# Four-layer graph and expert network on one core: the mask of an attention layer added by matmuls, its key and output rows handled in halves, and the order of the next layer's weight splits moved

## The reference, cut to what matters

```
x = x + gnn_L(layernorm(x));  x = x + ffn_L(layernorm(x))       (L = 0..3)
```

```
q, k, v = h @ Wq, h @ Wk, h @ Wv
score[t, s] = q[t] . k[s] / sqrt(64)     per head, for the edges s -> t; softmax over the edges of t
a = softmax-weighted sum of v;  o = a @ Wo
m = layernorm(h + o) * g1 + b1;  out = layernorm(m + relu(m @ W1 + b1') @ W2 + b2') * g2 + b2
```

## Time and profile before

| what | value |
|---|---|
| time, three runs | 580.49 us median (578.05 to 582.21) |
| the profiled execution | 578.05 us, of which its span is 576.3 us |
| TensorE busy | 549.3 us, 95% of the span |
| VectorE busy | 501.2 us, 87% |
| ScalarE busy | 428.2 us, 74% |
| GpSimd busy | 105.9 us, 18% |
| granted TensorE clock, mean | 0.997 of full speed |

### The profile page before, as it was taken

The page is one execution under the profiler, slowest core; times in us unless marked ns, Lnnn a source line. Parts: engine busy times, 40 slices in busy tenths (PEclk is TensorE's granted clock), DMA queues, the critical chain, the costliest instruction groups (busy, mean ns, idle before and its releaser), DMA issues.

```text
span 576.3 us, 8408 instructions
## 1 busy us (share of the span) xinstructions
PE 549.3 (95%) x2743; PEld 447.1 (78%) x2743; DVE 501.2 (87%) x486; ACT 428.2 (74%) x440; POOL 105.9 (18%) x82
## 2 busy tenths in 40 slices
PE   5898999999999999799999999999998999999997
PEld 4575888887688887588888888888877787888886
DVE  6789899897768886899999999999987769998996
ACT  5697898983268766978989899898843468878783
POOL 3132333000100003344343534410000200000000
PEclk9998999999999999999999999999999999999999
DMA  7889899998238885689999999999892258999920
GB/s 286 332 309 424 300 359 358 348 366 310 74 143 320 318 317 180 252 324 353 364 355 355 355 350 354 343 367 356 335 373 90 77 215 309 337 367 366 350 93 19
DMA packets 27978, 170.06 MB, mean 295 GB/s; under 512 B 5338, under 2 KB 5467, under 8 KB 7980
## 3 DMA queue, kind: packets, MB, share of 16 engines
q1 hardware_dynamic: 25986, 166.72, 76.3%
q10 hardware_dynamic: 1968, 3.04, 1.7%
HBM read 169.49 MB, written 0.26 MB: 295 GB/s over the span
## 4 chain that ended last, share of the span: by engine, by line
PE 80%; DVE 9%; ACT 6%; issue 3%; POOL 2%; DVEq 0%; POOLq 0%; ACTq 0%
PE y L678 34%; PE pre L678 33%; PE tp L684 5%; DVE w_lo L1068 4%; ACT w_hi L409 3%; PE wt L698 2%; PE y L779 1%; POOL rstd L345 1%; ACT L472 1%; DVE st L1015 1%; PE wt L909 1%; PE y L786 0%; PE tp L691 0%; PE pre L795 0%; ACT h L472 0%
## 5 line engine op out<-in xcount | busy, mean ns | idle before, releaser
L1068 DVE TENSOR_TENSOR w_lo<-raw,w_hi 128x2048 fp32r<-128x2048 f32 x151 | 354.2, 2368 | 31.9 <-ACT w_hi L409 30.7
L409 ACT ACTIVATE w_hi<-raw 128x2048 fp32r<-128x2048 f32 x152 | 287.7, 1916 | 0.0
L477 ACT ACTIVATE hT_hi<-tp 128x512 fp32r<-128x512 f32 x66 | 39.4, 598 | 58.2 <-PE tp L684 58.2
L678 PE MATMUL y<-w_hi,hT_hi 128*128 128x512 f32 x280 | 81.7, 413 | 0.0
L678 PE MATMUL pre<-w_hi,x_hi 128*128 128x512 f32 x292 | 79.7, 394 | 1.9 <-ACT x_hi L422 1.7
L678 PE MATMUL pre<-w_lo,x_hi 128*128 128x512 f32 x292 | 79.4, 394 | 1.2 <-DVE w_lo L1068 1.1
L678 PE MATMUL pre<-w_hi,x_lo 128*128 128x512 f32 x292 | 79.2, 393 | 0.2
L678 PE MATMUL y<-w_lo,hT_hi 128*128 128x512 f32 x280 | 75.8, 392 | 0.7 <-DVE w_lo L1068 0.6
L678 PE MATMUL y<-w_hi,hT_lo 128*128 128x512 f32 x280 | 75.2, 390 | 0.0
L678 PEld LDWEIGHTS pre<-w_lo,x_hi 128*128 128x128 f32 x292 | 55.1, 190 | 14.1 <-DVE w_lo L1068 1.9
L678 PEld LDWEIGHTS pre<-w_hi,x_hi 128*128 128x128 f32 x292 | 53.8, 188 | 14.8 <-issue 3.6
(11 more groups left out here) (267 smaller groups left out, 454.6 us busy)
## 6 DMA issues: line engine op xcount, KB each, us to landing
raw<-in_chunks SPq DMA_DIRECT2D x156, 1024.0 KB, 4.9
bias_wide<-in_L_ffn_b SPq DMA_DIRECT2D x4, 256.0 KB, 11.7
bias_wide<-in_L_ffn_b ACTq DMA_DIRECT2D x4, 256.0 KB, 6.3
side<-in_L_gnn_emb ACTq DMA_DIRECT2D x1, 512.0 KB, 4.1
affine<-in_L_ffn_W SPq DMA_DIRECT2D x1, 512.0 KB, 7.3
side<-in_L_ffn_W SPq DMA_DIRECT2D x1, 512.0 KB, 10.2
affine<-in_L_gnn_ln_g ACTq DMA_DIRECT2D x2, 256.0 KB, 5.8
affine<-in_L_gnn_ln_b ACTq DMA_DIRECT2D x2, 256.0 KB, 7.4
```

The source lines that it names most:

```text
L409: act.activation(w_hi[:, g % SPLIT_SLOTS], raw[:, g % RAW_SLOTS], ACT.Copy).then_inc(w_hi_ready, 4)
L477: act.activation(hT_hi[:, (s - 1) % 2], tp[:].rearrange("p (c n) -> p c n", n=P), ACT.Copy).then_inc(hT_hi_ready, 1)
L678: last = pe.matmul(dst, xs[:, k], ws[:, k], start=start and i == 0, stop=stop and i == len(passes) - 1, skip_group_check=seeded)
L1068: dve.tensor_tensor(w_lo[:, i], raw[:, g % RAW_SLOTS], w_hi[:, i].bitcast(F32), ALU.subtract).then_inc(w_lo_ready, 4)
```

## The change

What it does: (1) VectorE adds epsilon to the variance, behind `bn_aggr`, in every norm, and GpSimd only takes the power. (2) The number of clock keepers at layer 1's graph norm goes from 30 to 20. (3) q is scaled by 1/8 when ScalarE copies it; the mask `pen`, now float32r, is put into the two score banks by one matmul each with a float32r identity, and the score matmuls add to it; VectorE takes maximum and difference straight from the banks, which are now `pre[0]` and `wt[0]`. (4) k is copied, turned and copied back in two halves of columns, into two banks; the 6 keepers behind it are gone. (5) The score matmuls stand inside the v product, behind its first 4 matmuls. (6) The second bank of attended rows is divided in two halves, and the rows are turned, rounded and split by halves; the 3 keepers there are gone. (7) VectorE no longer splits parts of F between the scores and the attended rows: F's first quarter is split behind the last division, the other three behind the remainder of the turned rows, F+1 whole behind the first norm, and F+2 behind the last. (8) ScalarE rounds the second half of F+1 and both of F+2 ahead of the turned sum, not behind it. (9) One 128x128 copy for the float32r identity, in layer 1.

```diff
-BRIDGE = {"l0g": 0, "l0f": 0, "l1g": 30, "l1f": 37, "l2g": 23, "l2f": 30, "l3g": 28, "l3f": 14}
+BRIDGE = {"l0g": 0, "l0f": 0, "l1g": 20, "l1f": 37, "l2g": 23, "l2f": 30, "l3g": 28, "l3f": 14}
...
-                pool.wait_ge(sm("var"), nth("var", tag))
-                link(pool.tensor_scalar(rstd[:, 0:1], mv[:, 1:2], LN_EPS, None, ALU.add))
+                pool.wait_ge(sm("var_eps"), nth("var", tag))
...
-            act.activation(h[:, 0], pre[0][:], ACT.Copy).then_inc(sm("l3g_q"), 1)
+            act.activation(h[:, 0], pre[0][:], ACT.Copy, scale=DK ** -0.5).then_inc(sm("l3g_q"), 1)
             act.wait_ge(chunk_done, G_L3G + 2)
-            act.activation(h[:, 1], pre[1][:], ACT.Copy).then_inc(sm("l3g_k"), 1)
+            for cols in COL_HALVES:
+                act.activation(h[:, 1, cols], pre[1][:, cols], ACT.Copy).then_inc(sm("l3g_k"), 1)
...
-            round_turned("l3g_aT", tp, hT_hi[:, 0], "l3g_aThi")
+            round_halves("l3g_aT", hT_hi[:, 0], "l3g_aThi")
             round_half(G_L3F + 1, 0)
+            round_half(G_L3F + 1, 2)
+            round_half(G_L3F + 2, 0)
+            round_half(G_L3F + 2, 2)
             round_halves("l3g_midT", XT, "l3g_midTs")
-            round_half(G_L3F + 1, 2)
             act.wait_ge(sm("l3g_f1"), 1)
             act.activation(fT[0:32, :], ms[0:32, 0:P], ACT.Relu, bias=l3b1[:, 0:1]).then_inc(sm("l3g_f1s"), 1)
-            round_half(G_L3F + 2, 0)
-            round_half(G_L3F + 2, 2)
...
-            pe.wait_ge(sm("l3g_k"), 1)
-            turn(y[1], h[:, 1], sm("l3g_kT"))
-            keep_clock(6)
-            pe.wait_ge(sm("l3g_qTs"), 1)
-            pe.wait_ge(sm("l3g_kTs"), 1)
-            for j in range(HEADS // 2):
...
-            product(G_L3G + 2, y[0][:], x_hi, x_lo, True, True)
+            pe.wait_ge(sm("ident_r"), 1)
+            for dst in scored:
+                pe.matmul(dst[:].rearrange("p (c n) -> p c n", n=P), ident_r[:],
+                          pen[:].unsqueeze(1).broadcast_to([P, 4, P]), start=True, stop=True)
+            for part in range(2):
+                pe.wait_ge(sm("l3g_k"), part + 1)
+                for c in range(2):
+                    col = (2 * part + c) * P
+                    last = pe.transpose(k_turned[part][:, c * P:(c + 1) * P], h[:, 1, col:col + P], ident[:])
+                last.then_inc(sm("l3g_kT"), 1)
+
+            def scores():
+
+                pe.wait_ge(sm("l3g_qTs"), 1)
+                for j in range(HEADS // 2):
+                    if j % 2 == 0:
+                        pe.wait_ge(sm("l3g_kTs"), j // 2 + 1)
...
+            product(G_L3G + 2, y[0][:], x_hi, x_lo, True, True, between=scores)
...
-            pe.wait_ge(sm("l3g_a"), 2)
-            turn(tp, h[:, 0], sm("l3g_aT"))
-            keep_clock(3)
-            pe.wait_ge(sm("l3g_aThi"), 1)
-            product(G_L3G + 3, pre[1][:], hT_hi[:, 0], hT_lo[:, 0], True, True, low=(sm("l3g_aTlo"), 1))
+            for part in range(2):
+                pe.wait_ge(sm("l3g_a"), part + 2)
+                turn_half(h[:, 0], part, sm("l3g_aT"))
+            product(G_L3G + 3, pre[1][:], hT_hi[:, 0], hT_lo[:, 0], True, True, low=(sm("l3g_aTlo"), 2),
+                    high=(sm("l3g_aThi"), 1))
...
                 dve.bn_aggr(mv[:], st[:]).then_inc(sm("var"), 1)
+                dve.wait_ge(sm("var"), nth("var", tag))
+                dve.tensor_scalar(rstd[:, 0:1], mv[:, 1:2], LN_EPS, None, ALU.add).then_inc(sm("var_eps"), 1)
...
+            dve.tensor_copy(ident_r[:], ident[:]).then_inc(sm("ident_r"), 1)
...
-            dve.wait_ge(sm("l3g_kT"), 1)
-            dve.tensor_copy(scratch[:, 3 * D:4 * D], y[1][:]).then_inc(sm("l3g_kTs"), 1)
-            split_part(G_L3F, 0, 2)
+            for part in range(2):
+                dve.wait_ge(sm("l3g_kT"), part + 1)
+                dve.tensor_copy(scratch[:, 3 * D + part * 2 * P:3 * D + (part + 1) * 2 * P],
+                                k_turned[part][:, 0:2 * P]).then_inc(sm("l3g_kTs"), 1)
...
-                link(dve.scalar_tensor_tensor(out=S[:, hs], in0=chunks4(pre[p]), scalar=DK ** -0.5,
-                                              in1=pen[:].unsqueeze(1).broadcast_to([P, 4, P]), op0=ALU.mult,
-                                              op1=ALU.add))
-                link(dve.reduce_max(row[:, 0, hs], S[:, hs], AX_X))
-                dve.tensor_tensor(S[:, hs], S[:, hs], row[:, 0, hs].unsqueeze(2).broadcast_to([P, 4, P]),
+                link(dve.reduce_max(row[:, 0, hs], chunks4(scored[p]), AX_X))
+                dve.tensor_tensor(S[:, hs], chunks4(scored[p]), row[:, 0, hs].unsqueeze(2).broadcast_to([P, 4, P]),
                                   ALU.subtract).then_inc(sm("l3g_centred"), 1)
...
-                dve.tensor_tensor(h[:, 0].rearrange("t (j p d) -> t p j d", p=2, d=DK)[:, p], sums[:, :, 0:DK],
-                                  row[:, 3, hs].unsqueeze(2).broadcast_to([P, 4, DK]), ALU.mult).then_inc(
-                    sm("l3g_a"), 1)
-                split_part(G_L3F, 2 + p, 1)
-            low_turned("l3g_aThi", tp, hT_hi[:, 0], hT_lo[:, 0], "l3g_aTlo")
-            split_part(G_L3F + 1, 0, 2)
+                weighed = h[:, 0].rearrange("t (j p d) -> t p j d", p=2, d=DK)[:, p]
+                for js in [slice(0, 4)] if p == 0 else [slice(0, 2), slice(2, 4)]:
+                    dve.tensor_tensor(weighed[:, js], sums[:, js, 0:DK], row[:, 3, hs][:, js].unsqueeze(2).broadcast_to(
+                        [P, js.stop - js.start, DK]), ALU.mult).then_inc(sm("l3g_a"), 1)
+            split_part(G_L3F, 0, 1)
+            low_halves("l3g_aThi", hT_hi[:, 0], hT_lo[:, 0], "l3g_aTlo")
+            split_part(G_L3F, 1, 3)
...
-            split_part(G_L3F + 1, 2, 2)
+            split_part(G_L3F + 1, 0, 4)
...
-            split_part(G_L3F + 2, 0, 1)
...
-            split_part(G_L3F + 2, 1, 1)
             normalise_x("l3f")
-            split_part(G_L3F + 2, 2, 2)
+            split_part(G_L3F + 2, 0, 1)
             low_x("l3f")
+            split_part(G_L3F + 2, 1, 3)
             split_part(G_L3F + 3, 0, 4)
```

More of the change, by code:

```diff
@@ L175, in gnn_ffn_kernel @@
         agg2 = sb("agg2", [P, P])
-        pen = sb("pen", [P, P])
+        pen = sb("pen", [P, P], F32R)
+        ident_r = sb("ident_r", [P, P], F32R)
         mat_a = sb("mat_a", [P, P])
@@ L219, in gnn_ffn_kernel @@
         turned = [tp, wt[0]]
+        k_turned = [y[1], ms]
+        scored = [pre[0], wt[0]]
         landed = [sm(f"landed{i}") for i in range(RAW_SLOTS)]
@@ L661, in _, with product @@
         def _(pe):
-            def product(g, dst, xs_hi, xs_lo, start, stop, it=None, seeded=False, low=None, high=None):
+            def product(g, dst, xs_hi, xs_lo, start, stop, it=None, seeded=False, low=None, high=None, between=None):
                 hi, lo = w_hi[:, g % SPLIT_SLOTS], w_lo[:, g % SPLIT_SLOTS]
@@ L677, in product @@
                         pe.wait_ge(low[0], low[1])
+                    if i == KC and between is not None:
+                        between()
                     last = pe.matmul(dst, xs[:, k], ws[:, k], start=start and i == 0,
@@ L934, in _ @@
             turn(tp, h[:, 0], sm("l3g_qT"))
-            pe.wait_ge(sm("l3g_k"), 1)
-            turn(y[1], h[:, 1], sm("l3g_kT"))
-            keep_clock(6)
-            pe.wait_ge(sm("l3g_qTs"), 1)
-            pe.wait_ge(sm("l3g_kTs"), 1)
-            for j in range(HEADS // 2):
[L941 to L945, removed]
-            product(G_L3G + 2, y[0][:], x_hi, x_lo, True, True)
+            pe.wait_ge(sm("ident_r"), 1)
[13 more added lines that the diff above has]
+                        pe.wait_ge(sm("l3g_kTs"), j // 2 + 1)
+                    for p in range(2):
+                        rows = slice(p * DK, (p + 1) * DK)
+                        last = pe.matmul(scored[p][:, j * P:(j + 1) * P],
+                                         scratch[rows, 2 * D + j * P:2 * D + (j + 1) * P],
+                                         scratch[rows, 3 * D + j * P:3 * D + (j + 1) * P], start=False, stop=True,
+                                         skip_group_check=True)
+                last.then_inc(sm("l3g_scores"), 1)
+            product(G_L3G + 2, y[0][:], x_hi, x_lo, True, True, between=scores)
             def turn_exps(p):
@@ L1243, in graph_matrices @@
                     dve.memset(row[:, 5, :], 1.0)
-                    link(dve.tensor_scalar(pen[:], c_ds[:], 1.0, None, ALU.min))
-                    link(dve.tensor_scalar(pen[:], pen[:], -MASKED, MASKED, ALU.mult, ALU.add))
+                    link(dve.tensor_scalar(mat_b[:], c_ds[:], 1.0, None, ALU.min))
+                    link(dve.tensor_scalar(pen[:], mat_b[:], -MASKED, MASKED, ALU.mult, ALU.add))
                     link(dve.tensor_scalar(row[:, 3, 3:4], scal[:, 2:3], 1.0, None, ALU.add))
```

## The result

| | before | changed |
|---|---|---|
| median of 12 runs each | 581.5 us (578.05 to 583.55) | 577.19 us (574.14 to 579.78) |
| ratio, with its 95% interval | | 0.994 (0.9917 to 0.9964) |
| profiled execution, span | 578.05 us, 576.3 | 576.84 us, 575.0 |
| mean granted clock of the profiled execution | 0.997 | 0.994 |

The forecast was 576.6 us with a range of 573.2 to 579.8 and a change of 0.7%. The measured change is 0.6%. It lies within 1%, as forecast, and its interval, 0.4% to 0.8% faster, lies clear of no change.

The account below looks back on a forecast made before the run. TensorE, busy 95% of the span at full clock, was taken to bound the kernel; only stretches between products could shorten. Terms 0.30 + 0.70 + 0.37 + 2.56 = 3.93 us put the median at 576.6 us, range 573.2 to 579.8.

Parts of the forecast that it names:

- Norms: Epsilon on VectorE: five norms on the chain gain 0.14 us each, 0.70 together; for all norms, ends 0 and 1.9.
- Layer 0's first: First norm of layer 0: GpSimd's whole add step goes, since the variance is long known; gain 0.30 us.
- The norm inside the attention: First norm in the attention: the power is held beside a two-SBUF-input VectorE operation and still ends 0.44 behind; gain 0.
- Layer 1's graph norm: 30 keepers cut to 20: turning starts about 0.5 us earlier, but x_lo limits the third pass; gain 0.37, ends 0.1 and 0.65.
- Scores: Attention scores ready when before (0.1 earlier to 0.5 later); VectorE's scale-and-mask pass goes on both banks, 1.44 us.
- Attended rows: Attention: the two divisions gain 0.67 us (ends 0.4 and 0.75); turning, rounding and product by halves gain 0.45.
- The halves in turn and rounding: Attended rows turned and rounded by halves up to the product: 4.02 us instead of 4.47, gain 0.45.
- The tail: Small feed-forward to layer 3's experts: XN about 1.05 us earlier, but unchanged keepers hold the stretch at 7.2; gain 0.
- if that last stretch gets shorter: Sign of being wrong: the 7.2 us from the small feed-forward to the turning of XN was to stay unchanged.
- The full count of the norms: Rival: norms count in full, 0.31 us each, and covers hold nothing back; 6.4 us gain, median 574.1; chance 0.18.
- Scores late: Rival: scores 0.5 us late, second exponential waits up to 0.6 for v; gain about 2.5, median 578.0; chance 0.15.
- The clock: Rival: fewer keepers let the clock fall, layer 1's products at 1.2 GHz; 2.1 us slower, median 582.6; chance 0.05.

## Why the prediction was right

- **The sum.** 3.93 us forecast; the stretches without layer 0 give 4.09, and the medians of 12 runs 4.3. The time was right by its terms, though one of them was too large by 0.26 and another, of 0.24, was left out. That these two cancel is luck, and so is an agreement within a few tenths: without the first and the last line the stretches give 3.6, and the medians of the spans at one clock differ by about 3 us (at 0.997) and about 4.3 (at 0.994).
- **Norms.** 0.14 forecast for each of five. Measured 0.13, 0.16, 0.14 and 0.16, and 0.18 to 0.22 at the attention's norm. Layer 0's first: 0.30 forecast, 0.34 measured in this pair of profiles, where the edges came early in both; where they come later, as in eleven of thirteen profiles, the term is worth nothing. The norm inside the attention: 0 forecast, 0.03 measured, with the power held back as reckoned; the run with epsilon alone shows the same. By the rule of the Trainium skill (page "SBUF — State Buffer", section "Who interferes with whom") the one that comes second is blocked for all of the other. The trace agrees that it is held, but not for all of its own length behind that: it ended 0.41 us behind VectorE's operation here and 0.42 with epsilon alone, less than its own 0.55.
- **Layer 1's graph norm.** 0.37 forecast, 0.25 measured. That x_lo takes over as the last wait was right: TensorE's weight loads for the third pass stand 0.25 us for it, and the gap ahead of the turning is 0.44. The third pass starts 1.92 us behind the first in before and 1.93 after; the prediction's 1.5 was a misreading that nothing else used. What the term missed is that a pass that starts from a wait pays a start of its own, 1.17 us against the 1.07 of the earlier trace rows.
- **Scores.** Ready when they were: 3.38 forecast as unchanged, 3.37 measured. The pass that goes is 1.44 forecast and 1.46 measured at the second exponential (7.60 to 6.14).
- **Attended rows.** This is the mis-sized term: "Gain 0.67, ends 0.4 and 0.75" for the two divisions. It is 0.41: the lead of 1.46 at the second exponential is 1.87 when the rows can be turned. The last division before ends at 439.47, 12.00 behind the copy of k; in the changed kernel the turning starts at 439.05, when half of the second bank is divided; with the same 0.04 from end to turning as before, that half ends at 439.01, 10.13 behind the copy. I let the second bank's small steps follow the first division at once. TensorE's second weighing ends later, 0.21 us of waiting; the run with the splits back prices the split at 0.30 and not at 0.67. The halves in turn and rounding were forecast at 0.45; from the end of the division to o it is 4.08 against 4.49, 0.41.
- **The tail.** Right that XN comes 1.1 us early (5.95 us behind the addition and not 7.06) and that the keepers then hold it. Wrong was that the stretch stays at 7.2: it is 6.88 and not 7.12, and "if that last stretch gets shorter" was among the prediction's own signs of being wrong. The keepers did not stand without a gap up to the turning. TensorE's weight loads waited 0.24 us for XN in the kernel before, and no longer after, as the first load of the turning shows in each:

```profile
458.38 0.20 PEld L691 LDWEIGHTS tp<-ident,XN 128*128 128x128 f32 x2 [0.24 <-DVE XN L1035]
...
457.13 0.25 PEld L696 LDWEIGHTS tp<-ident,XN 128*128 128x128 f32 x2
```

  So XN was the last wait there, and a faster norm pays until the keepers take over: 0.24, which epsilon alone gave too (6.87). With 5 keepers 0.87 more comes out.
- **Rivals.** The full count of the norms would have shown 0.31 for each; it shows 0.13 to 0.22. Scores late: they were not, and v was in time: its copy ended 0.14 us ahead of the second exponential (434.88 and 435.02), about the 0.2 that I gave it. The clock: no dip in this profile where the 10 keepers were taken, a short one some 20 us behind in two of ten profiles, and 9.5 us where 80 are left out. The prediction's other sign of being wrong, products at a lower clock, did occur, but in layer 0, where the kernel before has such products too.

## What to carry to other kernels

A chain between engines is priced by its own steps, one by one, and by whichever engine is next to be late: a split that stands between two divisions costs only what the other engine's work does not cover, and keepers that were cut to fit a chain hold it as soon as the chain gets shorter. Retune the number of fillers after every change that shortens what they cover. Where the clock of single runs scatters the time by more than the change, compare stretches between the same two events, and do so at the same clock.

## What the runs showed of the hardware that was not expected

- A product of layer 0 loses about 1.6 us to a clock of 1.2 GHz in every profile without a filler there (before: 4.45 and not 2.84 us). Layer 0's graph part takes 19.9 to 20.0 us in four profiles of the changed kernel and its variants and 17.2 to 17.3 in six, with the same instructions up to there. Twelve transposes in the 1.5 us gap remove the first, but in both profiles that have them the clock fell earlier, between 17 and 36 us.
- Without 80 keepers of 0.115 us each, 9.2 us of work that nobody reads, the stretch that held them and what follows up to layer 2's experts takes 9.5 us longer than in the changed kernel, in the one run made.
- A chain's row can show keepers up to the very start of the next transpose (452.96 and 5.42 us, to 458.38) while the weight loads show 0.24 us of waiting in the same place. The loads' rows tell what is waited for.
